# Cross-attention of a decoder layer: G's last piece moved ahead of the attended sum, two buffers for the transposed context, low parts of rows on GpSimd, and reads of a context ahead of its transposes

## The reference

```python
x = layernorm(x + self_attn(x))        # one head of 256, 16 batches
Q = x @ Wq.T + bq;  K = ctx @ Wk.T + bk
attn = softmax(Q @ K.T / sqrt(1024))
x = layernorm(x + attn @ ctx)          # the attended sum is over the context itself
h = silu(x @ Wg) * (x @ Wu)            # Wg, Wu, Wd: 4-bit weights, dequantised
x = layernorm(x + h @ Wd)              # 2752 hidden columns
```

## Time and profile before

| | us |
|---|---|
| median of 3 runs | 1940.22 |
| lowest and highest run | 1939.06, 1947.41 |
| the profiled execution's own time | 1943.58 |
| its span, first to last instruction | 1941.9 |
| mean granted TensorE clock, share of full | 0.984 |
| TensorE busy | 1823.8 (94% of the span) |
| VectorE busy | 885.2 (46%) |
| ScalarE busy | 429.2 (22%) |
| GpSimd busy | 351.9 (18%) |

### The profile page before, as it was taken

One profiled execution on the slowest core, in us unless ns is written; L12 is line 12 of the kernel. 1 busy time (PEld: TensorE's weight loads), 2 busy tenths in 40 slices (PEclk: granted clock), 3 DMA queues, 4 the chain that ended last, 5 costly groups with the idle time before them and its releaser, 6 DMA issues.

```text
span 1941.9 us, 26602 instructions
## 1 busy us (share of the span) xinstructions
PE 1823.8 (94%) x10186; PEld 1021.9 (53%) x10186; DVE 885.2 (46%) x1342; ACT 429.2 (22%) x660; POOL 351.9 (18%) x262
## 2 busy tenths in 40 slices
PE   4988899888889869999999999999999999999998
PEld 2666644577777734445444544544445444444443
DVE  5688541668778864443444344344434310111111
ACT  3222210435454422222222222222222200000000
POOL 0222377112222211111111111112111100000000
PEclk9999999999899979999999999999999999999999
DMA  9242761489999953112211211221121322221220
GB/s 309 74 145 86 188 186 43 97 179 233 223 235 246 221 102 70 40 38 51 43 44 34 59 37 41 46 47 44 34 57 31 98 93 82 101 101 54 98 101 22
DMA packets 298807, 196.02 MB, mean 101 GB/s; under 512 B 258368, under 2 KB 272768, under 8 KB 296580
## 3 DMA queue, kind: packets, MB, share of 16 engines
q1 hardware_dynamic: 292516, 192.19, 39.6%
q10 hardware_dynamic: 6240, 3.15, 0.6%
HBM read 105.11 MB, written 50.34 MB: 80 GB/s over the span
## 4 chain that ended last, share of the span: by engine, by line
PE 52%; issue 31%; DVE 8%; POOL 4%; DMA 4%; ACT 1%; SPq 1%; POOLq 0%; DVEq 0%; ACTq 0%
PE psum L1289 50%; DMA arena<-in_x 2%; POOL arena L1016 2%; POOL arena L951 1%; PE psum L1498 1%; POOL small L942 1%; DVE arena L715 1%; PE psum L1516 1%; DMA x_parts_scratch<-arena 1%; DVE arena L403 1%; DMA arena<-in_L_xattn_Wq 1%; DVE small L684 1%; DVE arena L830 1%; DVE arena L495 1%; DVE small L410 0%
## 5 line engine op out<-in xcount | busy, mean ns | idle before, releaser
L1289 PE MATMUL psum<-arena 128*128 128x448 f16 (+8 forms) x9404 | 1754.3, 348 | 58.6 <-POOL arena L1016 15.9
L1289 PEld LDWEIGHTS psum<-arena 128*128 128x128 f16 (+4 forms) x9404 | 975.3, 107 | 818.7 <-issue 106.2
L1050 POOL TENSOR_TENSOR arena<-arena 128x1024 f16<-128x1024 f32 (+1 forms) x64 | 136.1, 2126 | 675.5 <-ACT arena L1231 675.5
L883 DVE SCALAR_TENSOR_TENSOR arena<-psum,small,arena 128x448 f32<-128x448 f32 x84 | 57.4, 684 | 409.1 <-PE psum L1289 409.1
L924 DVE SCALAR_TENSOR_TENSOR arena<-psum,small,arena 128x512 f32<-128x512 f32 x28 | 21.0, 751 | 327.4 <-PE psum L1289 315.6
L942 POOL TENSOR_TENSOR small<-small 112x1 f32<-112x1 f32 (+1 forms) x46 | 35.9, 781 | 585.4 <-DVE small L384 585.3
L1231 ACT ACTIVATE arena<-arena 128x1024 f16<-128x1024 f32 (+1 forms) x65 | 68.7, 1057 | 278.1 <-DVE arena L869 278.1
L1244 ACT ACTIVATE arena<-arena 128x448 f16<-128x448 f32 (+1 forms) x88 | 50.7, 577 | 291.9 <-DVE arena L883 291.9
L1016 POOL TENSOR_TENSOR arena<-arena 128x224 f16<-128x224 f32 x64 | 61.8, 966 | 144.8 <-ACT arena L1150 144.8
L889 DVE TENSOR_TENSOR arena<-arena 128x448 f16<-128x448 f32 (+1 forms) x88 | 55.0, 625 | 57.5 <-ACT arena L1244 57.5
L867 DVE TENSOR_TENSOR arena<-arena,psum 128x1024 f32<-128x1024 uint32 x65 | 79.4, 1221 | 2.6
(11 more groups left out here) (181 smaller groups left out, 745.9 us busy)
## 6 DMA issues: line engine op xcount, KB each, us to landing
h_scratch<-arena SPq DMA_DIRECT2D x84, 224.0 KB, 2.9
arena<-h_scratch SPq DMA_DIRECT2D x13, 1376.0 KB, 6.0
arena<-in_ctx SPq DMA_DIRECT2D x32, 512.0 KB, 4.5
arena<-in_x SPq DMA_DIRECT2D x32, 448.0 KB, 5.6
x_scratch<-arena SPq DMA_DIRECT2D x32, 448.0 KB, 3.5
arena<-in_L_ffn_down_qweight SPq DMA_DIRECT2D x21, 512.0 KB
x_parts_scratch<-arena SPq DMA_DIRECT2D x16, 448.0 KB, 5.5
arena<-in_ctx SPq DMA_DIRECT2D x16, 448.0 KB
```

The costliest lines, as they stand in the source:

```text
L883: dve.scalar_tensor_tensor(h_f[0:n, :], up[0:n, :], sc_u[0:n, :], g_act[0:n, :], ALU.mult, ALU.mult).then_inc(s_hf, 1)
L1050: pool.tensor_tensor(dst[1], src, dst[0], ALU.subtract).then_inc(s_wl, 1)
L1289: mm = pe.matmul(out, a, r, start=(k == 0), stop=(k == len(pairs) - 1))
```

## The change

In words:

- TensorE: one more piece of G, number KC, ahead of the loop. Batch n makes pieces KC+4n+1 to KC+4n+4 in place of KC+4n to KC+4n+3: two behind the logits, one behind `probs_t`, and the last behind `largest_of_context`. So the last piece that `logits(n+1)` needs stands ahead of `attended(n)`. The loop is unrolled on TensorE.
- Two buffers for the transposed context: `cxt` becomes a list, the second lying where `xtp` was. The transposes of context n+1 wait for `logits(n-1)`, not `logits(n)`.
- x1 transposed goes into the space of `x2t`. Its first pair is loaded only once M is done, pairs 1 to 4 ahead of the loop, pairs 5 to 7 in batches 0 to 2.
- `x2_lo` goes from VectorE to GpSimd, with contiguous operands: ScalarE's `x2_hi` now makes a float32 copy in the permuted order, and from that the high part in a second instruction. `x2p` has one buffer in place of two.
- VectorE: `normalise(n-1)` and two of the three `context_lo(n+1)` come ahead of `softmax_in(n)`, the third behind it; `row_term` writes its unused product to PSUM and no longer waits for the store.
- ScalarE: the three `context_hi` stand together, followed by the `g_out` of the piece just made.
- SyncE's queue: the three reads of context n+2 come ahead of the three transposes of context n+1.

The core of the diff:

```diff
@@ vector
-                if not known(n, 2):
-                    dve.wait_ge(s_lo, n - 1)
-                dve.tensor_tensor_reduce(yo[0:S, b % 2, :], xr3[0:S, b % 2, :], u_b[0:S, :], 1.0, 0.0,
+                dve.tensor_tensor_reduce(psum[0:S, 0:D], xr3[0:S, b % 2, :], u_b[0:S, :], 1.0, 0.0,
...
             def cross_attention(g, more):
                 for b, n, has in batches(g, more):
+                    if not known(n, 1):
+                        normalise(n - 1, (b + 3) % GB, n + 1 if has(1) else None)
+                        if has(1):
+                            context_lo(n + 1, (b + 1) % GB, 1)
                     softmax_in(n, b)
-                    if not known(n, 1):
-                        normalise(n - 1, (b + 1) % 2, n + 2 if has(2) else None)
-                    else:
+                    if has(1) and not known(n, 1):
+                        context_lo(n + 1, (b + 1) % GB, 2)
+                    if has(2):
                         context_max(n + 2, 0)
+                    if has(1):
+                        row_term(n + 1, (b + 1) % GB)
+                    probs_lo(n)
                     if has(2):
                         context_max(n + 2, 1)
...
@@ gpsimd
+            def x2_lo(n):
+                pool.wait_ge(s_hi, n + 1)
+                pool.tensor_tensor(x2p[0:S, 1, :], x2f[0:S, :], x2p[0:S, 0, :], ALU.subtract).then_inc(s_lo, 1)
+
...
                     if has(2):
-                        for k in range(4):
+                        for k in range(3):
                             g_lo(KC + 4 * n + k, 4 * (b % 2) + k, 1 - b // 2)
+                    if not known(n, 1):
+                        x2_lo(n - 1)
+                    if has(2):
+                        g_lo(KC + 4 * n + 3, 4 * (b % 2) + 3, 1 - b // 2)
@@ scalar
+            def x2_hi(n, b):
                 act.wait_ge(s_n, NB + n + 1)
+                if not known(n, 1):
+                    act.wait_ge(s_lo, n)
+                act.activation(x2f[0:S, :].rearrange("p (c q) -> p c q", c=KC),
                                yo[0:S, b % 2, :].rearrange("p (q c) -> p c q", c=KC), ACT.Identity,
+                               scale=XS).then_inc(s_x2f, 1)
+                if not known(n, 1):
+                    act.wait_ge(s_x2t, 16 * n)
+                act.wait_ge(s_x2f, n + 1)
+                act.activation(x2p[0:S, 0, :], x2f[0:S, :], ACT.Identity).then_inc(s_hi, 1)
@@ tensor
+            def cross_attention(n):
+                b = n % GB
+                logits(n, b)
+                if n + 2 < NB:
+                    g_chunk(KC + 4 * n + 1)
+                    g_chunk(KC + 4 * n + 2)
+                probs_t(n)
+                if n + 2 < NB:
+                    g_chunk(KC + 4 * n + 3)
+                attended(n, b)
+                if n + 2 < NB:
+                    largest_of_context(n + 2)
+                if n + 3 < NB:
+                    g_chunk(KC + 4 * n + 4)
@@ sync
             next_ctx(1)
+            sp.wait_ge(s_m, KC)
...
+            load_x1t(0)
+            sp.wait_ge(s_ub, 1)
+            for c in range(CC):
+                load_cxt(c, 0)
+            for q in range(1, 5):
+                load_x1t(q)
...
+            def cross_attention(g, more):
+                for b, n, has in batches(g, more):
+                    for c in range(CC):
+                        if has(1):
+                            sp.wait_ge(s_cl, CC * (n + 1) + c + 1)
+                        if has(2):
+                            load_ctx(n + 2, c)
+                        if c == 0 and not known(n, 1):
+                            store_x2(n - 1, (b + 1) % 2)
+                    if has(1):
+                        if not known(n, 1):
+                            sp.wait_ge(s_l, n)
+                        else:
+                            sp.wait_ge(s_v, 2 * NG)
+                        sp.sem_inc(s_due, 1)
+                        for c in range(CC):
+                            load_cxt(c, (b + 1) % 2)
...
                     if not known(n, 1):
+                        load_x2t(n - 1)
+                    if has(2):
                         sp.wait_ge(s_y3, 2 * (n + 1))
                         load_residual(n + 2, (b + 2) % GB)
+                    if known(n, 3):
+                        load_x1t(5 + n)
```

More of the change, by code:

```diff
@@ L293, in decoder_layer @@
         s_cx = [sem(f"ctx_chunk{c}_in") for c in range(CC)]
-        s_ct = sem("ctxT_in"); s_due = sem("ctxT_due")
+        s_ct = [sem(f"ctxT_slot{i}_in") for i in range(2)]; s_due = sem("ctxT_due")
         s_g = sem("g_in_psum"); s_ge = sem("g_copied"); s_re = sem("row_term_ready")
@@ L301, in decoder_layer @@
         s_y3 = sem("sum3_ready"); s_hi = sem("x2_hi_ready"); s_lo = sem("x2_lo_ready")
-        s_x2t = [sem(f"x2T_slot{i}_in") for i in range(2)]
+        s_x2t = sem("x2T_in"); s_x2f = sem("x2_f32_permuted")
         s_qw = [sem(f"qw_in{i}") for i in range(2)]; s_tc = [sem(f"tabc_in{i}") for i in range(2)]
@@ L749, in normalise @@
                 if beside is not None:
-                    context_max(beside, 0)
+                    context_lo(beside, (b + 2) % GB, 0)
                 norm_apply(y, NB + n, s_n)
@@ L1054, in _ @@
             inverse_std(2 * NB - 1, S)
+            x2_lo(NB - 1)
             def chunk(i, s, more):
@@ L1225, in high_part @@
                 if kind == 2:
-                    for i in range(2):
-                        act.wait_ge(s_x2t[i], 16 * (NB // 2 + 1))
+                    act.wait_ge(s_x2t, 16 * NB)
                 src = wbuf[kind]
@@ L1470, in _ @@
                         mm.then_inc(s_g, 1)
-            for y in range(2, KC):
-                pe.wait_ge(s_ge, y - 1)
-                g_chunk(y, 0)
+            for k in range(2, KC + 1):
+                g_chunk(k)
             pe.wait_ge(s_ube, 1)
-            cross_attention(0, True)
-            with pe.Fori(1, NG - 1) as g:
-                cross_attention(g, True)
-            cross_attention(NG - 1, False)
+            for n in range(NB):
+                cross_attention(n)
             def free_banks(q):
@@ L1526, in chunk @@
                     if t == 3:
-                        for k in range(2):
-                            pe.wait_ge(s_x2t[k], 16 * (NB // 2 + 1))
+                        pe.wait_ge(s_x2t, 16 * NB)
                     pe.wait_ge(s_hf, 4 * i + t + 1)
@@ L1549, in _ @@
             gather_gu(1, 1, 0, 0)
-            for i in range(2):
-                pe.wait_ge(s_x2t[i], 16 * (NB // 2 - 1))
+            pe.wait_ge(s_x2t, 16 * (NB - GB))
             with pe.Fori(0, NI // 2 - 1) as e:
@@ L1678, in _ @@
                          z_bf[1]).then_inc(s_tabo, 16)
-            for i in range(2):
-                sp.wait_ge(s_x1o[i], 16 * (GB // 2 + 1))
-            sp.wait_ge(s_v, 2 * NG)
-            for m in range(GB):
-                load_x1t(m, m)
             self_attention(NG - 1, False, False)
```

146 lines of the change are left out of this document (45 added, 101 removed).

## The result

| | before | after |
|---|---|---|
| median of the runs beside each other, us | 1940.22 (1938.6 to 1947.41, 5 runs) | 1929.76 (1924.06 to 1931.77, 5 runs) |
| profiled execution: own time, span, us | 1943.6, 1941.9 | 1929.76, 1928.0 |
| mean granted clock | 0.984 | 0.986 |

The ratio is 0.9931, with a 95% interval of 0.9913 to 0.9949: 10.5 us faster, where 17 was forecast. Measured once more among the experiments it gave 0.9922 (0.9902 to 0.9941). The forecast is made for the median; of the profiled executions' own times the difference is 13.8, since that of before lay 3.4 above its median.

What follows compares the result with a forecast made beforehand. It took a chain of waits through the context's transposes to set an 18.8 us period, above TensorE's 17.8. First batches 0, loop +21.9, tail -4.2: 17.7 us off 1940.2 gives 1922.5, say 1923; range 1909 to 1939.

Steps and rivals of the forecast that it cites:

- TensorE's wait for GpSimd goes: Even logits in cross-attention: eight waits of 2 us for G's low part vanish, with `x2_lo` on GpSimd in time.
- The period, 18.8 us: Cross-attention loop, logits to logits: 18.8 us a batch in place of 21.0, so ten periods from batch 4 gain 21.9 us.
- the chain: Logits, softmax, third `context_lo`, last read, three transposes, landing, next logits: 18.8 us a batch, said to set the period.
- The check: Bytes a batch, 4.89 MB minus one x1 transpose of 0.46 MB, at 233 GB/s: 19.0 us a batch.
- x1's transposes out of the loop: SyncE's queue: eight more transposes at 2.6 us, 21 us, ahead of the loop, no loss there; batches 0 to 2 carry pairs.
- The first four batches, 0: Up to logits(4): no gain; logits(1) at 410, logits(2) at 429, two periods of 22, logits(4) at 473, before 473.4.
- The tail, -4.2 us: Logits(14) to logits(15) takes 19.2 us where it took 15.0, the rest the same: a loss of 4.2 us.
- VectorE -32, GpSimd +34, clock above 0.96: Signs of being right: VectorE's busy time down 32 us, GpSimd's up 34, granted clock in the cross-attention stage above 0.96.
- TensorE as the bound: Rival, 17%: three transposes take 7.12 us, the chain is 17.1, TensorE's 17.8 us becomes the period: 1913 us.
- Slow transposes (9.53): Rival, 18%: the three transposes take 9.53 us with 2.8 landing, a period of 20.1 us: 1936 us.
- The transfers hold the period at 21.0: Rival, 9%: the low part's wait goes but the period stays 21.0 us, and only the tail's loss remains: 1944 us.
- The slower clock: Rival, 6%: logits waiting over 2 us for context lowers the clock, logits takes 5.7 us, period 22.0: 1955 us.

Runs made afterwards that it cites:

- b2: The changed kernel with G's last piece back behind the attended sum and no piece ahead of the loop: 1943.1 us, 0.9993 of the kernel before.
- a2: The changed kernel with the third `context_lo` moved ahead of softmax on VectorE: 1929.75 us, 0.9921 of the kernel before.
- b4: The changed kernel with the reads of contexts 2 to 15 fetching only 512 of 1024 columns: 1911.24 us, 0.9834 of the kernel before.
- b1: The changed kernel with x1's transposed pairs 2 to 7 back in batches 0, 2, ... 10: 1941.35 us, 0.999 of the kernel before.
- c2: The changed kernel with x1's pairs 5 to 7 in batches 4, 6, 8 instead of 0, 1, 2: 1937.55 us, 0.9964 of the kernel before.
- a3: The changed kernel with the transpose of context chunk 0 issued ahead of the read of chunk 2: 1940.39 us, 0.9983 of the kernel before.

## Why the prediction was right, and where it was off

The sign is right and the time is in the range, 7 us above the forecast. That it came so near is in part luck: the loop gave 6.5 us less than forecast and the tail 5.9 more, and the two errors stand in separate terms of the sum. Of the stage's own 17.7 us there came 15.7: 6.5 less by the period, 1.4 less by the first batches, 5.9 more by the tail; 2.35 were lost ahead of the stage. By its steps:

**TensorE's wait for GpSimd goes: right.** No wait for L1006 is left, and `x2_lo` is in time. GpSimd in batch 7 of the changed kernel:

```profile
546.14 0.61 POOL L1006 TENSOR_TENSOR arena<-arena 128x224 f16<-128x224 f32 x1 [2.45 <-ACT arena L1149]
549.24 2.13 POOL L1010 TENSOR_TENSOR arena<-arena 112x1024 f16<-112x1024 f32 x1 [2.48 <-ACT arena L1168]
551.33 0.61 POOL L1006 TENSOR_TENSOR arena<-arena 128x224 f16<-128x224 f32 x1
```

Logits(7) starts at 535.67, so `x2_lo` starts at L+13.6 and ends at L+15.7 (worked out: 13.8 and 15.9), for 2.13 us to the digit; the last `g_lo` is over at L+16.3, ahead of 17.8, since it took 0.61 and not the 1.88 us allowed for. b2 shows the wait's worth when this part is undone. The other wait that was to go, for `probs_lo`, went in the loop (4.0 us in four waits before, one of 0.68 us in the ten periods after) and stayed in batches 2 and 3 and in the tail.

**The period, 18.8 us: off by 0.65, the term that was mis-sized.** Its parts measured over the ten batches: start of the transposes behind logits 8.03 us (7.8 in the sum; two batches with a logits of 10.3 us have 9.3), three transposes 9.13 (8.8), landing 2.29 (2.2). Ten times 19.45 - 18.8 is 6.5 us. The placing of each step is right, as batch 7 shows: 7.8, 9.02, 2.4. What was wrong is the cause behind it. The prediction called the chain the bound and 233 GB/s a check; a2 shows that the chain can be cut by 1.7 us without any gain, b4 that bytes taken away bring 10 us, b1 that bytes put back cost 16. The length of the transposes is no constant of the chain: it is what the rate leaves them. The check was the better sum, and it had a slip of its own: it took off one transpose of x1 in each batch, but the kernel before issues eight in the ten (four pairs), so 48.9 - 3.7 = 45.2 MB at 233 GB/s are 19.4 us a batch, for 19.45 measured. With that the period's gain would have been put at 15.8 us and the median at 1929.

**x1's transposes out of the loop: right in kind,** and the largest part: b1. It was argued by queue time, and the runs say the same of bytes. The 18.9 of 21.0 us issued count one of four waits of the queue; all four are 23.2 us in the same eight batches, so 18.1. A pair cost 4.9 us in c2, as its queue time (4.9) says, and 4.0 in b1, as its bytes say (0.92 MB at 232 GB/s), where it held the queue for 5.1; no run separates the two.

**The first four batches, 0: right, by other means than told.** -1.4 us measured. Logits(1) was at 411.6 for 410, then came 19.3, 24.7 and 21.5 us for 19 and "two periods of 22". What the prediction left out: a pair of x1 in the queue makes the next context read late (5.09 us), VectorE stands in `context_max` for it, and `probs_lo` waits behind that, so TensorE pauses 3.33 us ahead of the attended sum (at 445.49 above). VectorE and SyncE's queue in batch 2:

```profile
442.53 1.22 DVE L682 TENSOR_REDUCE small<-arena 128x1 f32<-128x1024 f32 x1 [5.09 <-DMA arena<-in_ctx]
443.67 1.22 DVE L665 CUSTOM_DVE_ANT_0 psum<-arena 112x1024 f32<-112x1024 f32 x1
...
444.81 0.63 DVE L719 SCALAR_TENSOR_TENSOR arena<-psum,arena 128x112 f16<-128x112 f32 x3
```

```profile
431.74 6.05 SPq L1631 DMA_TRANSPOSE arena<-x_parts_scratch  x2
437.83 0.58 SPq L1691 DMA_DIRECT2D arena<-in_ctx  x1
```

**The tail, -4.2 us: wrong, it gained 1.7.** Four terms failed. First, the time before was misread. The prediction gave logits(14) to (15) 15.0 us, with the slow part of the row at 694.03 put down to logits(15). The slow part was the attended sum ahead of it, and logits(15) starts 1.7 us later, 16.7 us behind logits(14). TensorE's timeline of the kernel before, window 700.1 to 703.9 us:

```profile
699.92 3.98 PE L1289 MATMUL psum<-arena 128*112 128x375 f16 x24
```

Second, the transposes of the last context were given 8.4 us from the earlier trace rows; with no read beside them they took 7.07. Third, logits(14) was given the slow 5.68 us of the earlier trace rows; it took 4.03 behind a longer pause (2.75 us). So logits(14) to (15) is 16.45 us, not 19.2. Fourth, the rest, called "the same", was 1.5 us shorter (31.12 - 16.45 = 14.67, for 716.11 - 699.92 = 16.19 before): the last attended sum waited 1.33 us for the low part of its probabilities, where it had waited 2.52 with `normalise` ahead of that on VectorE, and took 6.62 us for 7.08.

**VectorE -32, GpSimd +34, clock above 0.96.** 857.5 us is 27.7 less; the 16 `x2_lo` of 2.0 us are gone, what came back of it was not broken down. The row term to PSUM costs 1333 ns in cross-attention for 1469, below even the lower bound of 0. GpSimd has 42.3 more: `inverse_std` took 15.0 more, unforeseen (last section), and the low parts of G 5.6 less. The clock is 0.98. TensorE's waits for the context are 1.7 us on average, above "0.5 to 1.5", which is the period's miss seen from the other side: 19.45 - 17.8.

**The rivals.** TensorE as the bound is what b4 comes near to, at 1911, and needs 0.77 MB a batch less. Its 7.12 us of the transposes was held possible only with an empty queue; the kernel before has 7.06 and 7.02 us in its loop too, ahead of logits(9) and (11). Slow transposes (9.53) did not come true in the mean but in single batches (8.51 to 10.72). "The transfers hold the period at 21.0" was right in its first half: they hold it, at 19.45, because x1's bytes left. The slower clock decided little here (two slow rows of logits, behind which the transposes began 1.7 us later), but is part of what b2 pays.

**The figure of 261 GB/s.** The Trainium skill's 261 GB/s for transposes ("DMA: Bandwidth & Descriptors", "Latency and other measured facts") is not met by the rows of three transposes: 3 x 0.52 MB in the 9.13 us that they hold the queue are 172 GB/s with the other transfers beside them, and 222 GB/s in the 7.07 us of the tail, less if the 2.3 us of landing are counted. The row was the right choice for the sum.

## What to carry to other kernels

Where the share of the transfers is above 1 and GB/s is flat across the stage, work out the period from the bytes first and let the chain of waits say only where the pause will be seen; starting such a transfer earlier only stretched it here, and moving transfers out of the loop is what paid, into a place where the queue is idle. When two limits lie within a few per cent of each other, undo each part alone: here each of two parts was, by the median, worth nothing without the other. In one in-order queue the place of a read behind a transpose matters more than any of this (77 us), since a transpose holds the queue while it is issued (4.79 us in a3, where a plain read took 0.37).

## What the runs showed that was not expected

**A transpose takes what it is given.** The same three transposes took 7.07 us with no read beside them in the tail, 7.8 with half the context reads, 9.0 to 9.1 in the loop, 10.7 when started 1.7 us earlier, 11.9 where eight transposes of x1 and the reads stood directly ahead (at 392.56, ahead of the loop's second batch). The queue issues nothing else in that time.

**A tiny GpSimd operation can wait a whole VectorE instruction out.** `inverse_std` works on 112 x 1 elements and took 0.55 us before (mean 552 ns of 15 in this stage). Beside a `context_lo` it takes 1.56 (mean 1485 ns of 15), and VectorE's apply behind it waits 6.9 us in these 15, 0.44 in the one shown. GpSimd and VectorE in batch 6 to 7:

```profile
536.09 1.56 POOL L932 TENSOR_TENSOR small<-small 112x1 f32<-112x1 f32 x1 [2.54 <-DVE small L386]
```

```profile
535.96 1.28 DVE L713 SCALAR_TENSOR_TENSOR arena<-arena,small 128x1024 f16<-128x1024 f32 x1
537.69 0.81 DVE L397 TENSOR_SCALAR arena<-arena,small 112x1024 f32<-112x1024 f32 x1 [0.44 <-POOL small L932]
```

VectorE's instruction ends at 537.24 and GpSimd's at 537.65. By the Trainium skill, "SBUF — State Buffer", "Who interferes with whom", a VectorE instruction with two SBUF inputs contends with a GpSimd instruction that reads SBUF. The trace agrees: the one operation reads SBUF, the other has two inputs there, and GpSimd's ends 0.41 us behind VectorE's. Here it costs VectorE 6.9 us, on an engine with time to spare. A rule that the prediction weighed for the operation that was moved bore on one that was not.

**The clock behind a pause.** In the changed kernel the rows of logits and two pieces of G behind pauses of 2.17 and 2.62 us took 10.31 us for 8.63, those behind 2.73 and 1.99 us took 8.63. In b2 those behind 2.09, 2.94, 2.95, 3.19 and 3.55 us took 10.1 to 10.3, that behind 3.07 us 8.60. The length of the last pause alone does not tell it, and no run here separates what does.
